# Order of the first packs, place of the first values and of a clear, and a later half of one pack set, in an attention and expert kernel

## What is computed

```
# x: (16, 256, 128), ctx: (16, 1601, 128), 16 heads of 8
q  = einsum('bnd,hde->bhne', layernorm(x), Wq)
k  = einsum('bmd,hde->bhme', ctx, Wk)
v  = einsum('bmd,hde->bhme', ctx, Wv)
att = softmax(q @ k.T * 0.125)                 # over the 1601 keys
x  = x + tanh(g_xattn) * (concat_heads(att @ v) @ Wo.T)
# then 8 experts, 2 per token, 128 -> 512 -> 128, gelu
x  = x + tanh(g_ffn) * moe(layernorm(x))
```

## Time and profile before

| | us |
|---|---|
| median of 3 runs | 1359.2 (1354.61 to 1360.03) |
| the profiled execution's own time | 1349.07 |
| its span | 1347.3 |
| PE busy | 1285.8 (95%) |
| DVE busy | 1157.3 (86%) |
| ACT busy | 1097.5 (81%) |
| POOL busy | 544.2 (40%) |
| mean granted TensorE clock | 0.976 |

### The profile page before, as it was taken

The page is one execution under the profiler, slowest core; times in us unless marked ns, Lnnn a source line. Parts: engine busy times, 40 slices in busy tenths (PEclk is TensorE's granted clock), DMA queues, the critical chain, the costliest instruction groups (busy, mean ns, idle before and its releaser), DMA issues.

```text
span 1347.3 us, 38009 instructions
## 1 busy us (share of the span) xinstructions
PE 1285.8 (95%) x14041; PEld 627.1 (47%) x14041; DVE 1157.3 (86%) x2268; ACT 1097.5 (81%) x2190; POOL 544.2 (40%) x1208
## 2 busy tenths in 40 slices
PE   4899999999999999999999999999999999999992
PEld 2233444444444444444444444444444443389982
DVE  7879999999999999999999999999999999546434
ACT  1468898988888889898988989898988888966661
POOL 3212526262625253535444443526262603136542
PEclk7789999999999999999999999999999999999996
DMA  3232121212121212122222212121211110088886
GB/s 92 78 89 79 45 68 50 71 49 76 40 85 35 65 53 64 57 61 63 59 67 59 65 55 68 51 70 48 71 48 48 42 56 11 16 281 250 263 264 236
DMA packets 61077, 112.67 MB, mean 84 GB/s; under 512 B 13052, under 2 KB 36476, under 8 KB 60748
## 3 DMA queue, kind: packets, MB, share of 16 engines
q1 hardware_dynamic: 54043, 97.67, 24.6%
q0 software_dynamic: 4320, 8.99, 2.0%
q10 hardware_dynamic: 2529, 3.58, 0.8%
HBM read 52.77 MB, written 13.71 MB: 49 GB/s over the span
## 4 chain that ended last, share of the span: by engine, by line
PE 74%; DVE 18%; issue 3%; SPq 2%; DMA 1%; ACT 1%; POOL 0%; POOLq 0%; DVEq 0%
PE pv L820 27%; DVE mx L1545 15%; PE st L771 14%; PE mxp L793 13%; PE st L1037 5%; PE mxp L1047 5%; PE st L878 4%; PE st L887 3%; PE st L899 1%; PE st L850 1%; PE st L922 1%; PE st L862 1%; PE st L932 1%; DVE x_sb L1740 1%; SPq L407 1%
## 5 line engine op out<-in xcount | busy, mean ns | idle before, releaser
L1545 DVE TENSOR_REDUCE mx<-mxp 128x2 f32<-128x804 f32 x1024 | 985.3, 989 | 70.8 <-PE mxp L793 60.9
L1076 ACT ACTIVATE arena<-st 128x512 f32<-128x512 f32 (+1 forms) x1664 | 891.6, 595 | 85.6 <-PE st L771 78.7
L820 PE MATMUL pv<-arena 128*32 128x256 f32 x6656 | 534.0, 393 | 0.4 <-ACT pv_sb L1083 0.4
L793 PE MATMUL mxp<-kpack,qpack 48*128 48x402 bf16 x2048 | 456.4, 344 | 15.5 <-DVE mx L1545 14.1
L771 PE MATMUL st<-qpack,kpack 51*128 51x256 bf16 (+1 forms) x3328 | 448.8, 273 | 2.6 <-DMA qpack<-mxT 2.4
L771 PEld LDWEIGHTS st<-qpack,kpack 51*128 51x128 bf16 (+1 forms) x3328 | 199.2, 96 | 202.2 <-ACT arena L1076 108.5
L793 PEld LDWEIGHTS mxp<-kpack,qpack 48*128 48x128 bf16 x2048 | 142.7, 93 | 164.8 <-DVE mx L1545 90.8
L820 PEld LDWEIGHTS pv<-arena 128*32 128x32 f32 x6656 | 131.5, 108 | 176.5 <-ACT arena L1076 87.9
L658 POOL CAST mxs<-nmx 128x8 bf16<-128x8 f32 x64 | 12.2, 191 | 265.5 <-DVE nmx L1553 265.3
L1217 ACT ACTIVATE arena<-st,bias 128x256 f32<-128x256 f32 (+1 forms) x172 | 74.9, 437 | 45.1 <-PE st L1037 41.6
L691 POOL DMA_INDIRECT rows<-xrow,pos x64 | 66.0, 1031 | 95.2 <-DVE pos L1402 80.0
(11 more groups left out here) (194 smaller groups left out, 903.3 us busy)
## 6 DMA issues: line engine op xcount, KB each, us to landing
kpack<-ksp SPq DMA_DIRECT2D x750, 50.0 KB
arena<-in_w12T SPq DMA_DIRECT2D x43, 576.0 KB
arena<-in_ctxT SPq DMA_DIRECT2D x15, 800.5 KB, 4.6
qpack<-qsp SPq DMA_DIRECT2D x187, 32.0 KB
xblk<-rows SPq DMA_DIRECT2D x28, 132.0 KB, 3.9
rows<-in_pads SPq DMA_DIRECT2D x8, 264.0 KB
arena<-results SPq DMA_DIRECT2D x8, 256.0 KB, 7.0
arena<-results ACTq DMA_DIRECT2D x8, 256.0 KB, 7.4
```

The lines of the kernel that those rows point to most:

```text
L793: eng.matmul(mxp[pair % MX_BUFS][:, rg, 0:WIN], qpack[rows, b % 2, g * JJ + jj, t * P:(t + 1) * P], kpack[rows, b % 2, g * JJ + jj, WSTART ...
L820: ins = eng.matmul(pv[32 * j:32 * j + 32, 0:N], vaug[0:n, b % 2, kt, at:at + 32], pt[0:n, (2 * u + rg) % PT_BUFS, jj * N:(jj + 1) * N], st ...
L1076: eng.activation(pt[0:n, c % PT_BUFS, :], ring[bank_of["S", u, p]][0:n, :], ACT.Exp, scale=SCALE).then_inc(s_exp, 1)
L1545: eng.tensor_reduce(mx[:, tj, w, :], mxp[windows_done % MX_BUFS][:, :, 0:WIN], AX.X, ALU.max).then_inc(s_red, 1)
```

## The change

Four edits, all of which concern the first batch or what stands ahead of it.

1. `first_packs`: the three query packs of kind 0 (parts 0, 1, 4) are issued behind the three key packs of kind 0, as soon as ACT has written kind 0 of the queries (`s_qhi`), ahead of the key packs of kinds 1 and 2. It holds for SP's row group 0 and for ACT's row group 1.
2. The two memsets of `vaug` move from DVE (behind the ranks, ahead of the first reduction) to POOL, between the layernorm of batch 0 and that of batch 1.
3. Batch 0's value tiles are made one by one behind windows 7 to 16 and 18 to 20 on PE. ACT copies the first two banks behind the twelve key packs that it issues, the last two behind the placing of group 0's maxima.
4. Of the twelve key packs of batch 1's group 0, SP issues six at r = 14 as before, and the other six at r = 23, behind the maxima of group 2 and ahead of the 24 packs that stood there.

```diff
+V0_AHEAD = 7
@@ def first_packs
             for part in range(PARTS):
                 if K_KIND[part] == 0:
                     pack_key_rows(eng, 0, 0, part, rg)
+            eng.wait_ge(s_qhi, 1)
+            for part in range(PARTS - rg):
+                if Q_KIND[part] == 0:
+                    pack_query_rows(eng, 0, part, rg)
             eng.wait_ge(s_k3, NK)
             for part in range(PARTS):
                 if K_KIND[part] > 0:
                     pack_key_rows(eng, 0, 0, part, rg)
             eng.wait_ge(s_q3, 1)
             for part in range(PARTS - rg):
-                pack_query_rows(eng, 0, part, rg)
+                if Q_KIND[part] > 0:
+                    pack_query_rows(eng, 0, part, rg)
@@ SP, batch 0
                     elif r == 14:
-                        pack_keys(1, 0)
+                        pack_keys(1, 0, range(PARTS // 2))
                     elif r == 23:
+                        pack_keys(1, 0, range(PARTS // 2, PARTS))
                         pack_keys(1, 1)
                         pack_keys(1, 2)
@@ POOL
             norm("X", 0)
+            vparts = vaug[:, :, :, 0:VP * H].rearrange("p k t (h c) -> p (k t) h c", c=VP)
+            eng.memset(vparts[:, :, :, 0:VC], 0.0).then_inc(s_vone, 1)
+            eng.memset(vaug[:, :, :, VP * H:VW].rearrange("p k t w -> p (k t) w"), 0.0).then_inc(s_vone, 1)
             norm("X", 1)
@@ PE
-            def values(b, c):
+            def values(b, c, some=None):
                 i = bank_of["V", b, c]
                 t0, tn = VCH[c]
-                eng.wait_ge(*freed[i])
-                for t in range(tn):
+                some = range(tn) if some is None else some
+                if 0 in some:
+                    eng.wait_ge(*freed[i])
+                for t in some:
@@ PE, start
-            for c in range(NV - 1):
-                values(0, c)
             turn_rows("X", 1)
             queries(1)
             for n in range(issued(0, 0)):
                 if n == 1:
                     eng.wait_ge(s_xnT, 2)
                 maximum(*divmod(n, NMX))
-                if n == 0:
-                    values(0, NV - 1)
-                elif n == NMX + 1:
+                if n == NMX + 1:
                     turn_maxima(0)
+                elif n >= V0_AHEAD:
+                    t = n - V0_AHEAD - (n > NMX + 1)
+                    if t < KT:
+                        values(0, t // VCH[0][1], [t % VCH[0][1]])
@@ ACT, start
             copy_rows(1)
-            for c in range(NV - 1):
-                copy_values(0, c)
             first_queries(1)
-            copy_values(0, NV - 1)
             eng.wait_ge(s_id, 16)
...
             for g in range(1, NG - 1):
                 for part in range(PARTS):
                     pack_key_rows(eng, 0, g, part, 1)
+            for c in range(NV // 2):
+                copy_values(0, c)
             copy_maxima(0)
             eng.wait_ge(s_mxT, 1)
             place_half(eng, 0, 1)
+            for c in range(NV // 2, NV):
+                copy_values(0, c)
@@ DVE, start
-            eng.memset(vparts[:, :, :, 0:VC], 0.0).then_inc(s_vone, 1)
-            eng.memset(vaug[:, :, :, VP * H:VW].rearrange("p k t w -> p (k t) w"), 0.0).then_inc(s_vone, 1)
```

## The result

The changed kernel takes 1364.45 us (median of 15 runs, 1360.46 to 1370.82), the kernel before, run beside it, 1359.07 (15 runs, 1354.61 to 1360.37). The ratio is 1.0037, with a 95% interval from 1.0025 to 1.0049: slower by some 5 us, where 0.5 faster was forecast. In a later comparison the same two kernels gave 1.0023 (1.0011 to 1.0034), 3.1 us. One execution of each there ran far outside all the others (4528.2 us of the changed kernel, 1538.49 of the kernel before), and the ratios leave these two out.

What follows compares the result with a forecast made beforehand. PE bounds the kernel (busy 95%), with gains only in the first hundred us, chiefly a 2.41 us hole at unit 26 from SP's queue. - 6.9 + 2.8 + 4.4 - 0.8 = - 0.5 us gave 1358.7, range 1350 to 1365.

Steps and rivals of the forecast that it cites:

- costed at nothing: Clears on POOL ahead of batch 1's seed: they fit into 6.34 us of idle time, so cost 0.
- 5.4 at most: Length of the clears on POOL, for 4108 elements at the rate of POOL's one-input cast.
- the named point, 6.34 us: POOL's idle time ahead of batch 1's seed; past it each us of clears delays everything.
- POOL's clears run past the seed: Rival, chance 0.10: at 9.7 us the clears make batch 1's layernorm and window 0 3.4 late; 2.9 slower, 1362.1.
- The sign set for it: POOL's seed step for batch 1 later than 16.5 would show the forecast wrong about the clears.
- The figure that the prediction did weigh: POOL's clears at 2.6 cycles an element: an estimated 8.9 us, window 0 2.6 later.
- put at 0.8 won: Batch 0's values between windows: 0.8 won, taken between 1.7 lost and 2.0 to 4.0 won.
- 1.7 was the bound: Value tiles between windows: 13 tiles hold DVE up by at most 13 x 0.13 = 1.7 us.
- That half of the term: Clock may rise before the units begin, as PE is nearly full: 2.0 to 4.0 us won.
- - 6.9 + 2.8 + 4.4 = + 0.3: Six packs later: 6.9 gained up to unit 39, then a new hole of 2.8 and half clock costing 4.4.
- The 5.0 us of clock that the forecast takes back at unit 26: Without the hole at unit 26, the 10.41 us behind it run at full clock and PE saves 5.0.
- the 6.8 us that the prediction took as its limit: Whole kernel: a change within 0.5% (6.8 us) is about what a measurement can't tell from none.

Runs made afterwards that it cites:

- set 2: Changed kernel whole (1363.58 us), with clears back on DVE, with values also back, and kernel before with clears early on POOL; kernel before beside them 1360.51.
- Edit 2 alone: Kernel before with only the two clears moved from DVE to POOL, between the layernorms: 1351.7 us, ratio 1.0022.
- Edit 1 alone: Kernel before with only the query packs of kind 0 put ahead of the later key packs: 1348.32 us, ratio 0.9996.
- The even deal: Kernel before with batch 1's key packs dealt 6, 24, 18 instead of 12, 24, 12 on SP: 1354.41 us, ratio 0.9958.

## Why the prediction was wrong

**Edit 2 was costed at nothing, and costs 2.9 to 3.7.** That is the first step that failed. The clears' length was bounded rightly (5.4 at most, 3.8 measured) and they do fit into POOL's idle time; the named point, 6.34 us, wasn't reached, so the rival "POOL's clears run past the seed" didn't come either. The sign set for it did, POOL's step at the seed later than 16.5 (18.68), but by another path. What I left out is the other engine. Batch 1's layernorm hangs on DVE's seed, which stands behind DVE's casts, and the cast stood still beside the clears on POOL: 3.0 more for one cast in the changed kernel, 3.8 in the kernel with this edit alone. The cover was looked for on the engine that got the work, not on the one beside it. The Trainium skill states the rule in "SBUF — State Buffer", section "Who interferes with whom": DVE's copies and casts can run in a mode that takes the port pair which it shares with GpSimd, and whichever engine has it keeps the other off for a whole instruction. The rows agree that the cast stands still beside a clear. That it gets no turn between two clears (3.43 and 0.40), nor between thirteen short ones in a row, goes beyond that sentence. The figure that the prediction did weigh, 2.6 cycles of 1.2 GHz an element in the Trainium skill, "GPSIMD Engine Reference", section 3.1, was not at work, as the prediction allowed, since the page puts it down to two inputs: 3.43 us for 3744 elements is 0.92 ns each, where 2.6 such cycles are an estimated 2.2.

**Edit 3 was put at 0.8 won, and costs 1.1 (alone, not clear of none) to 3.6.** That is the second step. Two terms were off. The tile was priced at 0.52 from four tiles in a row; alone between windows it takes 0.73, so a step is 1.18 and not 1.04, and the way to the first score grew by 2.6, where 1.7 was the bound. No run varied the number of tiles, so that the price makes the whole 2.6 rests on the rows. And the clock didn't come up before the units, though PE was busy 20.09 of 23.70: it stayed at half there in every profile with this edit. That half of the term was a guess at even odds, and should have stood in the range alone.

**Edit 4's mechanism came as told; its size was off by as much as edit 2's, the other way.** The hole at unit 26 gone, SP issuing group 3's maxima right behind 30 packs, a hole at unit 39 and the clock behind it. Forecast - 6.9 + 2.8 + 4.4 = + 0.3, measured - 2.4 alone (or - 4.2 together with edit 1 in set 2). The hole was 2.20 instead of 2.8 with the edit alone (1.68 and 1.39 in the two profiles of the changed kernel), the half clock 6.8 us long, so 3.4 instead of 4.4, and it doesn't always come: see below. The 5.0 us of clock that the forecast takes back at unit 26 don't always have to be paid before, either.

**Edit 1** at nothing was right.

**The sum.** Forecast 0 - 0.8 + 0.3 = - 0.5. In set 2 the same three terms are + 3.7 + 3.6 - 4.2 = + 3.1. The first comparison's + 5.4 is more; the two intervals, 1.0025 to 1.0049 and 1.0011 to 1.0034, overlap, and what makes the rest wasn't settled. Both intervals are 1.6 us to either side, so a comparison of this kernel tells much less than the 6.8 us that the prediction took as its limit. The time itself, 1364.45, is inside the range given, at its edge, and that is luck: the range reached so far for a slow clear and a long second slow stretch, and neither came.

## What to carry to other kernels

Before work is moved into another engine's idle time, look at what the engines that share something with it do in that very stretch, and what hangs on them. On POOL and DVE this is decided by which operations meet: beside the clear the cast took 3.35 instead of 0.37, while the sum with an input in PSUM took 0.56 (line 1576, at 10.13), and 0.57 behind it. So a clear goes where DVE makes no casts, best where it idles; beside DVE's reductions from PSUM no run here had one. When a queue is late at one place, work moved behind that place arrives at the next: sum the queue up to each deadline, and deal the work so that no place is late (here 6, 24, 18 for 12, 24, 12: six us).

## What the runs showed of the hardware that I had not expected

**The clock after a hole isn't the same each time, and what decides it isn't shown.** Of the two profiles of the changed kernel, one has 0.66 over the 10 us behind its hole of 1.68 us (the table above), the other, in set 2, full clock behind 1.39:

```profile
110.95:112.34 1.39, 0.00 (x0) 0.00 (x1) 1.24 (x2) 0.26 (x1) 0.00 (x0) 1.00 0.02 4
112.34:122.34 10.00, 9.43 (x108) 3.63 (x108) 7.53 (x12) 7.71 (x15) 2.56 (x8) 1.00 0.39 114
```

It also differs between kernels whose instructions around unit 26 are the same. Edit 2 alone, the hole at unit 26 and the 10 us behind it:

```profile
88.53:90.96 2.43, 0.00 (x1) 0.00 (x1) 1.79 (x2) 0.25 (x1) 0.00 (x0) 1.00 0.09 26
90.96:100.96 10.00, 9.73 (x106) 4.92 (x106) 7.34 (x15) 8.30 (x16) 0.78 (x4) 1.00 0.27 77
```

Edit 1 alone:

```profile
85.97:88.40 2.43, 0.01 (x2) 0.00 (x0) 1.80 (x2) 0.26 (x1) 0.00 (x0) 1.00 0.11 32
88.40:98.40 10.00, 9.99 (x92) 5.47 (x93) 5.78 (x13) 6.73 (x14) 0.78 (x4) 0.83 0.27 77
```

and the kernel before has 0.52 over 10.41 us behind its 2.41. So a hole of the same length (2.41 to 2.43) cost nothing in clock, 1.7 us and 5 us. The spread of the runs goes with the clock: the 15 runs of the changed kernel have mean clocks from 0.977 (1360.83 us) to 0.969 (1370.82), and 0.008 of 1365 us is 22 us more at half clock, which is worth 11, about the spread. The even deal, which has no such hole, has 2.5 us between its slowest and fastest run (6 runs), the kernel before beside it 5.5 (22 runs). One profile of a kernel with a hole therefore tells that the clock can fall there, not what it costs on average.

**A series of short writes on POOL shuts DVE's cast out as a long one and a short one behind it do** (4.51 us for a 0.37 us cast, in one profile of one kernel).

**The experts' stretch differs by 11 us from one set of runs to another** (140 and 151 us) with the same instructions, which is twice the effect that was looked for. Each set had a chip of its own, so chip and time of running aren't told apart.
